# Row-tiled 32-row strips for the first convolution and the middle product, x kept in natural order

## What is computed

```python
x = x + conv1d(x, W0, taps=9, groups=4) + cond @ cw0.T + side      # layer 0
x = x + (sum_k att1[b, k] * E1[k]) @ x + att1 @ bias_k1            # layer 1
x = x + (sum_k att2[b, k] * E2[k]) @ x + att2 @ bias_k2            # layer 2
x = x + conv1d(x, W3, taps=9, groups=4) + cond @ cw3.T + side      # layer 3
```

## Time and profile before

| | before |
|---|---|
| median of three runs | 2600.42 us |
| the profiled execution, its own time | 2600.42 us |
| its span | 2598.5 us |
| TensorE busy (matmuls), weight loads | 98%, 80% |
| VectorE, ScalarE, GpSimd busy | 88%, 80%, 0% |
| on-chip and off-chip transfers | 808.75 MB, 311 GB/s mean |

### The profile page before, as it was taken

The page is one execution under the profiler, slowest core; times in us unless marked ns, Lnnn a source line. Parts: engine busy times, 40 slices in busy tenths (PEclk is TensorE's granted clock), DMA queues, the critical chain, the costliest instruction groups (busy, mean ns, idle before and its releaser), DMA issues.

```text
span 2598.5 us, 38320 instructions
## 1 busy us (share of the span) xinstructions
PE 2554.9 (98%) x11082; PEld 2071.6 (80%) x11082; DVE 2277.4 (88%) x3384; ACT 2077.8 (80%) x1940; POOL 3.7 (0%) x17
## 2 busy tenths in 40 slices
PE   6999999999999999999999999999999999999997
PEld 4788888888888888888888888888888888888885
DVE  7988888888888888888888888888888888888884
ACT  4788878888887888888788888878888887888885
POOL 0000000000000000000000000000000000000000
PEclk8999999999999999999999999999999999999998
DMA  5788888888888888888888888888888888888875
GB/s 193 284 317 317 320 318 314 321 324 316 317 320 318 313 321 324 316 316 320 318 314 321 324 316 316 321 318 313 321 323 317 317 320 317 315 320 322 317 300 210
DMA packets 335448, 808.75 MB, mean 311 GB/s; under 512 B 37066, under 2 KB 40146, under 8 KB 302674
## 3 DMA queue, kind: packets, MB, share of 16 engines
q1 hardware_dynamic: 333200, 807.16, 83.5%
q10 hardware_dynamic: 2242, 1.53, 0.2%
HBM read 137.45 MB, written 134.22 MB: 105 GB/s over the span
## 4 chain that ended last, share of the span: by engine, by line
PE 97%; DVE 2%; issue 0%; DMA 0%; ACT 0%; ACTq 0%; SPq 0%; DVEq 0%
PE pair L766 82%; PE quad L810 14%; PE pair L800 1%; DVE mixed L595 0%; PE quad L747 0%; DMA x_in<-in_x 0%; DVE w_hi L528 0%; DVE weighted L583 0%; DVE x_lo L504 0%; DVE x_lo L630 0%; DVE x_hi L627 0%; DMA x_ph<-x_ch 0%; DVE x_ch L569 0%; DVE w_lo L534 0%; DMA x_ch<-x_ph 0%
## 5 line engine op out<-in xcount | busy, mean ns | idle before, releaser
L766 PE MATMUL pair<-x_hi,w_hi 128*128 128x512 f32 x3072 | 1227.1, 399 | 8.7 <-DVE x_lo L643 5.4
L766 PE MATMUL pair<-x_hi,w_lo 128*128 128x512 f32 x3072 | 1213.1, 395 | 0.0
L766 PE MATMUL pair<-x_lo,w_hi 128*128 128x512 f32 x3072 | 1209.0, 394 | 0.0
L766 PEld LDWEIGHTS pair<-x_hi,w_lo 128*128 128x128 f32 x3072 | 579.6, 189 | 137.3
L766 PEld LDWEIGHTS pair<-x_hi,w_hi 128*128 128x128 f32 x3072 | 579.0, 188 | 136.4 <-DVE x_lo L643 5.8
L766 PEld LDWEIGHTS pair<-x_lo,w_hi 128*128 128x128 f32 x3072 | 581.6, 189 | 131.5
L595 DVE TENSOR_REDUCE mixed<-weighted 128x128 f32<-128x1152 f32 x256 | 576.9, 2254 | 0.1
L402 ACT COPY x_out<-x_ch 128x1024 f32<-128x1024 f32 x256 | 530.3, 2073 | 2.9 <-DMA x_ch<-x_ph 2.9
L351 ACT COPY x_ch<-x_in 128x1024 f32<-128x1024 f32 x256 | 531.0, 2076 | 1.9 <-DMA x_in<-in_x 1.9
L410 ACT COPY x_ph<-pair 128x512 f32<-128x512 f32 x512 | 314.8, 615 | 272.1 <-PE pair L766 272.1
L418 ACT ACTIVATE x_ph<-pair,bias_now 128x512 f32<-128x512 f32 x512 | 358.6, 700 | 216.2 <-PE pair L766 216.2
(11 more groups left out here) (80 smaller groups left out, 607.2 us busy)
## 6 DMA issues: line engine op xcount, KB each, us to landing
x_ph<-x_ch SPq DMA_DIRECT2D x1024, 256.0 KB, 2.6
x_ch<-x_ph SPq DMA_DIRECT2D x1024, 256.0 KB, 2.6
x_in<-in_x SPq DMA_DIRECT2D x128, 1024.0 KB, 5.5
out<-x_out SPq DMA_DIRECT2D x128, 1024.0 KB, 4.2
x_out<-in_W SPq DMA_DIRECT2D x8, 144.0 KB, 5.4
expert<-in_e ACTq DMA_DIRECT2D x2, 512.0 KB, 8.0
x_ph<-in_e_t SPq DMA_DIRECT2D x1, 512.0 KB, 4.3
x_ph<-in_small ACTq DMA_DIRECT2D x1, 458.5 KB, 3.5
```

The costliest lines, as they stand in the source:

```text
L766: mm = nc.tensor.matmul(conv_bank[g % 2], w[l][:, m, g, :], x[:, g, m:m + N], start=(m == 0 and x is hi and w is w_hi), stop=(m == BLK - 1 ...
```

## The change

The three products, the order of the layers and the split in high and low parts stay. The layouts of two of them change:

- x is no longer cut in phases nor moved. It is loaded two samples ahead in channel rows, ScalarE rounds it as it lies (`high_x`), and x_hi and x_lo are [128 rows, 512 + 2 columns, 4 phases], with the phase innermost.
- Convolution 1 takes 12 strips of 32 rows (a group's channels) in place of 3 blocks of 128 rows: strip d = 4 x shift + q multiplies phase q of x, shifted by `shift` columns, by a 32 x 128 matrix. The moving operand is `x[rows_of(g), shift:shift + N, q]`: 512 elements with a step of four. The four groups use the four quarters of the rows and four banks, and are issued in turn: 144 matmuls.
- Its result is already in phase order by channel of the group, one bank a group, and is rounded and split straight out of the banks (`high_x1`, `low_x1`), without transfers.
- The middle becomes row-tiled too: for each group, product and phase a matmul with 32 rows, 48 in all. Its weights are needed by every quarter of the rows, so the matrix goes to DRAM in one transfer (`save_m`) and comes back in four (`spread_m`), one sample ahead.
- The middle's matrix is mixed by 16 `scalar_tensor_tensor` of 128 elements (`mix_experts`), the identity as the first addend; in place of 9 "experts" there are 8.
- x3's and x4's moves stay. bias4 is added in `join` instead of in `evacuate_x4`, evacuations work on halves of four banks, and the eight banks are two sets of four that alternate by sample.
- Convolution 4 has the same 36 matmuls; the last group waits for the matrix of two samples on to be copied out of its bank.
- The head is rebuilt accordingly: taps of convolution 1 come in four transfers, weights of the strips are zeroed by GpSimd and filled by VectorE; convolution 1 of sample 0 stands among the small network's products.

The diff, cut to its core:

```diff
-        x_hi = sb("x_hi", [C, G, N + 2 * HALO], f32r)
-        x_lo = sb("x_lo", [C, G, N + 2 * HALO], f32r)
+        x_hi = sb("x_hi", [C, N + 2 * HALO, PH], f32r)
+        x_lo = sb("x_lo", [C, N + 2 * HALO, PH], f32r)
+        x1_hi = sb("x1_hi", [C, G, N], f32r)
+        m_saved = nc.dram_tensor("m_saved", [ODD, C, 2, C], f32).ap()
+        m_rows = sb("m_rows", [C, ODD, G, 2, C], f32r)
...
@@ SP
+            def save_m(b, slot):
+                sp.wait_ge(m_split, b + 1)
+                sp.dma_start(m_saved[slot, :, :, :], m_pair[:, :, :].bitcast(f32)).then_inc(m_stored, DMA)
+            def spread_m(b, slot):
+                sp.wait_ge(m_stored, DMA * (b + 1))
+                for q in range(PH):
+                    sp.dma_start(m_rows[rows_of(q), slot, :, :, :].bitcast(f32),
+                                 m_saved[slot, :, :, :].rearrange("(g c) t o -> c g t o", g=G)
+                                 ).then_inc(m_spread, DMA)
...
+            def step(b, slot, first=False, load_next=True, last=False):
+                if not (first and slot == 0):
+                    move_x3(b - 1)
+                if load_next:
+                    load(b + 2, slot)
+                if not first:
+                    store(b - 2, slot)
+                if not last:
+                    save_m(b + 1, 1 - slot)
+                if not (first and slot == 0):
+                    move_x4(b - 1, 0)
+                if not last:
+                    spread_m(b + 1, 1 - slot)
+                if not (first and slot == 0):
+                    move_x4(b - 1, 1)
...
@@ ScalarE
+            def high_x(b, slot, turn):
+                act.wait_ge(x_loaded[slot], DMA * (turn + 1))
+                wait(act, conv1_done, G * b)
+                nc.scalar.copy(x_hi[:, HALO:N + HALO, :],
+                               x_in[:, slot, :].rearrange("c (n q) -> c n q", q=PH)
+                               ).then_inc(x_hi_ready, 1)
+            def high_x1(b, tile, half):
+                if half == 0:
+                    wait(act, mid_done, PH * b)
+                act.wait_ge(conv1_done, G * b + (half + 1) * G // 2)
+                nc.scalar.copy(halves(x1_hi, half), halves(tile, half)).then_inc(x1_high, 1)
...
@@ VectorE
+            def mix_experts(b):
+                for k in range(K):
+                    for l in range(2):
+                        if k == 0:
+                            wait(dve, m_done, b)
+                        else:
+                            dve.wait_ge(mix_ready[l], K * b + k)
+                        nc.vector.scalar_tensor_tensor(mixed[l][:, :], expert[l][:, k, :],
+                                                       mix[l][:, b, k:k + 1],
+                                                       ident[:, :] if k == 0 else mixed[l][:, :],
+                                                       ALU.mult, ALU.add).then_inc(mix_ready[l], 1)
...
+            def step(b, slot, first=False, load_next=True, last=False):
+                if not (first and slot == 0):
+                    split_x3(b - 1)
+                set_bias3(b)
+                if not first:
+                    set_bias4(b - 2)
+                for half in range(2):
+                    low_x1(b, banks[slot], half)
+                if not last:
+                    split_m(b + 1, banks[1 - slot])
+                    low_x(b + 1, 1 - slot)
+                if load_next:
+                    mix_experts(b + 2)
...
@@ TensorE
+            def conv1_strips(b, tile, strips):
+                for d in strips:
+                    shift, q = d // PH, d % PH
+                    for w, x in ((w0_hi, x_hi), (w0_hi, x_lo), (w0_lo, x_hi)):
+                        for g in range(G):
+                            mm = nc.tensor.matmul(
+                                tile[:, g, :], w[rows_of(g), d, :, :].rearrange("c q o -> c (q o)"),
+                                x[rows_of(g), shift:shift + N, q],
+                                start=(d == 0 and x is x_hi and w is w0_hi),
+                                stop=(d == STRIPS - 1 and w is w0_lo))
+                            if d == STRIPS - 1 and w is w0_lo:
+                                mm.then_inc(conv1_done, 1)
+            def conv1(b, tile):
+                pe.wait_ge(x_lo_ready, b + 1)
+                wait(pe, x4_ready, 2 * (b - 1))
+                conv1_strips(b, tile, range(STRIPS))
...
+            def middle(b, slot, tile):
+                pe.wait_ge(m_spread, DMA * G * (b + 1))
+                pe.wait_ge(x1_split, 2 * b + 2)
+                for g in range(G):
+                    for part, x in ((0, x1_hi), (0, x1_lo), (1, x1_hi)):
+                        for q in range(PH):
+                            mm = nc.tensor.matmul(tile[:, q, :], m_rows[rows_of(q), slot, g, part, :],
+                                                  x[rows_of(q), g, :],
+                                                  start=(g == 0 and part == 0 and x is x1_hi),
+                                                  stop=(g == G - 1 and part == 1))
+                            if g == G - 1 and part == 1:
+                                mm.then_inc(mid_done, 1)
+            def step(b, slot, last=False):
+                conv1(b, banks[slot])
+                if not last:
+                    pe.wait_ge(x3_ready, 2 * b)
+                    middle_matrix(b + 1, banks[1 - slot])
+                conv4(b - 1, banks[1 - slot], not last)
+                middle(b, slot, banks[slot])
```

More of the change, by code:

```diff
@@ L229, in wait, with halves @@
                 eng.wait_ge(s, value)
+        def halves(tile, half):
+            return tile[:, half * PH // 2:(half + 1) * PH // 2, :]
         block = ctx.enter_context(nc.Block())
@@ L310, in _ @@
-            with sp.Fori(1, (B - 4) // 2) as i:
+            sp.wait_ge(band_zeroed, 1)
+            taps = a["W1"].rearrange("c (k g o) -> c k g o", k=TAPS, g=G)
+            for p in range(PH):
+                rows, first = slice(p, PH * (GROUP - 1) + p + 1, PH), PH - 1 - p
+                sp.dma_start(band[rows, first:first + TAPS, :, :], taps).then_inc(taps1_placed, DMA)
+            save_m(0, 0)
+            spread_m(0, 0)
+            for b in range(ODD):
+                step(b, b, first=True)
@@ new lines, in step @@
+            def step(b, slot, turn, first=False, last=False):
+                if not first:
+                    for half in range(2):
+                        join(b - 2, slot, turn - 1, half)
+                for half in range(2):
+                    high_x1(b, banks[slot], half)
+                if not last:
+                    high_x(b + 1, 1 - slot, turn + slot)
+                if not (first and slot == 0):
+                    for half in range(2):
+                        evacuate_x4(b - 1, banks[1 - slot], half)
+                evacuate_x3(b, banks[slot])
@@ L460, in _ @@
             for b in range(B - ODD, B):
-                step(b, b % ODD, b // ODD, last=True)
+                step(b, b % ODD, b // ODD, last=(b == B - 1))
             for half in range(2):
                 join(B - 2, 0, B // ODD - 1, half)
-            for g in range(G):
-                evacuate_x4(B - 1, g)
+            for half in range(2):
+                evacuate_x4(B - 1, banks[0], half)
             for half in range(2):
@@ L690, in _ @@
[L690 to L703 removed]
+            dve.wait_ge(experts_loaded, 2 * DMA)
@@ new lines, in _ @@
+            dve.wait_ge(mix_copied, 4)
+            mix_experts(0)
+            for half in range(2):
+                low_x1(0, banks[0], half)
+            split_m(0, banks[1])
+            dve.wait_ge(bias_l_ready, 1)
+            carry_bias(0)
+            mix_experts(1)
+            carry_bias(1)
+            dve.wait_ge(bias3_done, 1)
+            nc.vector.tensor_copy(bias3_ch[:, :], early[2][:, 0:B]).then_inc(bias3_all, 1)
+            dve.wait_ge(bias3_all, 1)
+            set_bias3(0)
@@ L803, in middle @@
-            def middle(b):
-                wait(pe, x3_ready, 2 * b)
-                pe.wait_ge(m_split, 2 * b + 2)
-                for q in range(PH):
-                    pe.wait_ge(x1_split, PH * b + q + 1)
-                    for m, x in ((m_hi, x1_hi), (m_hi, x1_lo), (m_lo, x1_hi)):
-                        mm = nc.tensor.matmul(mid_bank[:, q, :], m[:, :], x[:, q, :],
-                                              start=(m is m_hi and x is x1_hi), stop=(m is m_lo))
-                    mm.then_inc(mid_done, 1)
```

692 lines of the change are left out of this document (265 added, 427 removed).

## The result

The changed kernel takes 3697.15 us (median of 4 runs, 3696.61 to 3697.86) against 2600.24 us before (2599.79 to 2600.62): a ratio of 1.4219, with a 95% interval of 1.4194 to 1.4243. It is 1097 us slower. The forecast was 5872 us, the range 3500 to 6260 us, and the middle of the first rival 3730 us.

The account below looks back on a forecast made before the run. TensorE's matmul stream was taken as the bound: 33.4 (convolution 1) + 8.4 (convolution 4) + 2.8 (middle) + 0.34 (matrix product) + 0.5 (tiling) = 45.4 us a sample, x 128, + 59 = 5870, forecast 5872 us; range 3500 to 6260.

Parts of the forecast that it names:

- What bounds the kernel: Whole kernel: TensorE's stream of matmuls sets the length, busy for 98% of the span; 128 samples of 19.84 us.
- the price of a strip set: Convolution 1: 36 sets of four matmuls, each reading 512 elements at 1.81 ns, 0.929 us a set, 33.4 us a sample.
- Rival 1: Convolution 1: the step slows reads by factor 2 to 2.2, sets 0.464 to 0.512 us, 3570 to 3950 us; chance 0.17.
- Rival 2: Convolution 1 and middle: the step is free, weight loads queue, 48 sets at 0.445 us, about 3965 us; chance 0.05.
- Rival 3: Strips and middle: strided read free, sets could reach 0.213 us, about 2485 us, or 2665 at 0.232; chance 0.11.
- Rival 4: Convolution 1 and middle: row tiles don't run side by side, 53.8 us a sample, 6950 us with free step; chance 0.05.
- Middle: Middle product: 12 sets of row-tiled matmuls at 0.232 us, 2.8 us a sample; 5.3 us if weight loads queue.
- convolution 4: Convolution 4's matmuls, untouched by the change: 8.4 us a sample.
- changes of tiling: TensorE's array changing between whole and row-tiled three times a sample: 0 to 0.5 us, taken as 0.5.
- VectorE and ScalarE: Their work falls to about 14 and 13 us a sample, beside TensorE's 45 us, and is costed at nothing.
- Head and tail: Start and end of the kernel, outside the 128 samples: 59 us, as in the kernel before.
- New waits: TensorE's waits for x1, matrix transfers, x3 and x_lo: all covered; x_lo about 8 us after convolution 1, under 11.2 us.

## Why the prediction was wrong, step by step

**What bounds the kernel** was right: TensorE before and after, 99% of the chain, and the 128-fold sample. The two splits of the time, into samples and into sets, carried over as worked.

**The step that failed is the price of a strip set.** I wrote "a new 16 bytes of a partition no sooner than every 1.8 ns, however much of them is used", and took 0.929 us, between 0.232 and 0.957. It measured 0.461 us. The difference is 36 x 0.468 = 16.8 us a sample, 2156 us, and the whole miss is 5872 - 3697 = 2175 us. What was wrong was carrying the lines' price to lone fp32r elements. Such a price exists: on TensorE bfloat16 pays 1.76 ns for each line, up to 0.90 us a matmul, and VectorE and ScalarE pay about 1.8 ns for an element with a step of 16 bytes. But in fp32r TensorE takes two elements in that time even out of two lines, and a full line's four. Three engines agreed on one number; that didn't show that TensorE takes one request at a time at that pace, and no row of before had a strided read by TensorE. The range held because both readings of "a step hurts" were in it.

**Slips in the working** that left the forecast as it was: ScalarE's fixed 160 ns doesn't follow from the 700 and 1134 ns that I named, which give 266 ns and so 1.77 ns an element in place of 1.87; the run with strips read contiguously has 2048 such elements in 3882 ns, and (3882 - 2076)/1024 = 1.76. The first rival's terms add up to 28.74 us a sample and 3740 us, not 3730. A multiply-add of 128 elements took 0.345 us, above the 0.28 that I called the most.

**Rival 1** (factor 2, 3730 us) came within 33 us (43 by the right sum) and within 1% of the set (0.464 against 0.461 us). Its reason isn't confirmed in full: the factor is 2 only at full clock. At half clock the same step costs 8%, so it is a time per element, as in the forecast, only half as long.

The Trainium skill's page "SBUF — State Buffer", Specifications (TRN2), asks for two hits in each 16-byte line. In fp32r the step of 8 bytes has two and still took 0.452 to 0.46 us, so the measurement decides against it; the "4 fp32" that the section on the DMA port swizzle of the same Trainium skill page calls a free stride fell with the 0.461 us of the kernel itself.

**Rival 2** fell: with contiguous operands strip sets took 0.2315 us and the middle's 0.230, where four queued loads would have taken 0.445. The Trainium skill's page "TensorE: Matmul & The Clock Gate", Part 3, lets a weight load overlap with running matmuls only where its row group is another one. The middle agrees: its four loads start within 0.11 us while the sets go on every 0.230 us. **Rival 3** fell for the strips as given. Its line, "faster as long as a set stays under 0.24 us", was wrong too, and at odds with its own 2665 us at 0.232: with sets at 0.23 us and the late bias mended, the kernel took 2649.77 us, slower than before. **Rival 4** fell: sets of four start together.

**Middle** 2.8 us, measured 2.87 with its entry; **convolution 4** 8.4, measured 8.53; **changes of tiling** 0.5 us, measured some 0.3 (28.35 less 16.6, 8.35, 2.77 and 0.34). I counted three a sample, and the trace has two, ahead of the matrix product and ahead of the middle; from the middle to the strips, both row-tiled, the next set starts 0.23 us on. **VectorE and ScalarE** about 14 and 13 us, measured 13.6 and 12.1 us a sample. **Head and tail** 59, measured 66.5.

**New waits** were right for the kernel as given and half right for what lies behind. I wrote that x_lo would come about 8 us after convolution 1 and that the cover was 3 us thin without slow strips. It came 6.7 us after it in the kernel as given (timeline of VectorE: 2016.65 us) and 14 us after it with contiguous strips, where rounding and splitting x with a step took 3.5 us more and the join stood 4 us in the way. What I had left out is the join: I priced it but didn't place it, ahead of the rounding of x1 on ScalarE and behind a bias that VectorE sets late.

## What to carry to other kernels

Where TensorE reads fp32r, keep at least whole 16-byte lines together: every pattern of less took 0.84 to 0.92 ns an element, about twice the time at full clock, in row tiles and whole arrays alike, while the reordering costs ScalarE and VectorE 2.0 and 1.6 us a sample that they had free. Price such a read from a run that has one on that engine and in that type; a step of 16 bytes took 0.46 us in fp32r and 0.90 us in bfloat16. And when a slow stage is made fast, look again at the order on the helpers: a four-microsecond join behind a late bias was free under it and cost 305 us without it.

## What was not expected of the hardware

- TensorE's read has a price per 16-byte line that depends on the type: bfloat16 1.75 to 1.77 ns a line, fp32r about 1.8 ns for a full line or for any two elements.
- Single fp32r elements 32 or 64 bytes apart took 0.43 us, less than 8 or 16 bytes apart (0.45 to 0.46). Why isn't known.
- At half clock a step of 8 or 16 bytes is nearly free (0.46 us against 0.43 contiguous).
- Four weight loads of 32 rows in different row tiles start within 0.11 us, and sets of four row tiles run at 0.230 us, no slower than one whole matmul (0.232).
- A bfloat16 matmul between two fp32r ones saved next to nothing (6 us in the kernel, 24 of them a sample); three in a row saved 0.026 us together.
